# Low parts of x before the second layer norm, GpSimd taking over small work, and the hidden layer's tail cast on ScalarE

## What is computed

```python
xn = layernorm(x)                                   # over the 256 features
# recurrent branch (D = L = 256, K = 4 taps)
y    = gelu(xn @ w_y + b_y)
xb   = xn @ w_x + b_x
conv = conv_b + sum_k conv_w[k] * shift(xb, K-1-k)
gate_x = sigmoid(conv @ w_ig + b_ig); gate_a = sigmoid(conv @ w_ag + b_ag)
log_a = -8 * gate_a * softplus(a_param); a = exp(log_a); mult = sqrt(1 - exp(2*log_a))
h[t] = a[t] * h[t-1] + gate_x[t] * conv[t] * mult[t]    # a = 0, mult = 1 at t = 0
attn = (h * y) @ w_out + b_out
# feed-forward branch, HIDDEN = 682; ternary(w): -s, 0 or s with s = mean |w|
ffn  = (silu(xn @ ternary(w1)) * (xn @ ternary(w3))) @ ternary(w2)
out  = x + attn + ffn
```

## Time and profile before

| what | us |
|---|---|
| median of 3 runs (lowest, highest) | 75.48 (75.25, 76.12) |
| the profiled execution, its own time | 75.99 |
| its span, first to last instruction | 74.2 |

### The profile page before, as it was taken

One profiled execution on the slowest core, in us unless ns is written; L12 is line 12 of the kernel. 1 busy time (PEld: TensorE's weight loads), 2 busy tenths in 40 slices (PEclk: granted clock), 3 DMA queues, 4 the chain that ended last, 5 costly groups with the idle time before them and its releaser, 6 DMA issues.

```text
span 74.2 us, 1064 instructions
## 1 busy us (share of the span) xinstructions
PE 69.2 (93%) x364; PEld 58.6 (79%) x364; DVE 61.2 (82%) x101; ACT 48.3 (65%) x75; POOL 31.5 (43%) x43
## 2 busy tenths in 40 slices
PE   4999969999999999999999999999999999999920
PEld 4985758877888888888888888888899999988800
DVE  4897499999999999999979974697960799999750
ACT  3674523899999999999998978466699910000000
POOL 6385647245851680016002979947689000000000
PEclk9999999999999999999999999999999999999999
DMA  0889999920000000000000000000000000000195
...
DMA packets 5095, 5.63 MB, mean 76 GB/s; under 512 B 525, under 2 KB 4578, under 8 KB 5090
## 3 DMA queue, kind: packets, MB, share of 16 engines
...
q10 hardware_dynamic: 144, 0.01, 0.1%
...
HBM read 4.51 MB, written 1.05 MB: 75 GB/s over the span
## 4 chain that ended last, share of the span: by engine, by line
PE 80%; DMA 7%; DVE 5%; SPq 3%; issue 1%; DVEq 0%
PE slot L664 25%; PE slot L647 23%; PE slot L696 14%; PE slot L706 8%; DMA x_sb<-x 7%; PE slot L767 4%; PE slot L673 2%; SPq L186 2%; DVE stats L436 2%; PE slot L740 2%; DVE x_sb L551 1%; PE slot L636 1%; DVE xt_lo L455 1%; SPq L183 1%; DVEq L52 0%
## 5 line engine op out<-in xcount | busy, mean ns | idle before, releaser
L256 POOL TENSOR_TENSOR g_lo<-w_raw,g_hi 128x512 fp32r<-128x512 f32 x10 | 14.1, 1421 | 9.0 <-ACT g_hi L338 8.9
L664 PE MATMUL slot<-xt_hi,w_q 128*128 128x512 f32 x40 | 15.7, 393 | 0.0
L664 PE MATMUL slot<-xt_lo,w_q 128*128 128x512 f32 x40 | 15.7, 393 | 0.0
L514 DVE SCALAR_TENSOR_TENSOR w_raw<-w_raw,s,slot 128x512 f32<-128x512 f32 x10 | 7.3, 747 | 3.1 <-ACT w_raw L332 3.0
L696 PE MATMUL slot<-w_q,g_hi 128*128 128x256 f32 x40 | 9.7, 283 | 0.0
L696 PE MATMUL slot<-w_q,g_lo 128*128 128x256 f32 x40 | 9.7, 283 | 0.0
L492 DVE SCALAR_TENSOR_TENSOR conv<-slot,par,conv 128x511 f32<-128x511 f32 (+2 forms) x12 | 9.0, 748 | 0.4
L664 PEld LDWEIGHTS slot<-xt_hi,w_q 128*128 128x128 f32 x40 | 7.5, 188 | 1.7
L664 PEld LDWEIGHTS slot<-xt_lo,w_q 128*128 128x128 f32 x40 | 7.5, 188 | 1.7
L332 ACT ACTIVATE w_raw<-slot,scale 128x512 f32<-128x512 f32 x10 | 6.6, 684 | 3.1 <-PE slot L664 3.1
L696 PEld LDWEIGHTS slot<-w_q,g_lo 128*128 128x128 f32 x40 | 7.7, 192 | 0.0
...
## 6 DMA issues: line engine op xcount, KB each, us to landing
...
```

The source lines that it names most:

```text
L256: nc.gpsimd.tensor_tensor(g_lo[:, j, s], g[:, n % RING], g_hi[:, j, s].bitcast(f32), ALU.subtract).then_inc(g_lo_set, 1)
L514: nc.vector.scalar_tensor_tensor(out=g[:, n % RING], in0=silu[:, n % RING], scalar=s32[:, 0:1], in1=slot[H_SLOT[s][j]][:, 1], op0=ALU.mult ...
L664: mm = nc.tensor.matmul(slot[H_SLOT[s][j]][:, o], w13_q[:, c, col:col + P], v[:, s, c], start=(c == 0 and v is xt_hi), stop=(c == KC - 1 a ...
```

## The change

- SyncE loads sequence 1's x in two transfers instead of one.
- VectorE does `xt_lo_of(0)` ahead of sequence 1's statistics, takes that sequence in two halves, and puts the first columns of the convolution (`first_columns`, with constants of their own, in place of the correction L488) between the two normalisations and ahead of the taps. It no longer sets the pads of gt, makes v_eps or a_rate, or casts the tail.
- GpSimd makes v_eps, fewer constants ahead of the first rstd, the high parts of w_ig and w_ag (`tensor_copy`), w_y's low part in two chunks after all of xn, the rates, the pads, and b_split's low part after lo_of_g(4).
- ScalarE loads gelu's table by a one-column gelu ahead of w_y's high part, no longer makes the high parts of w_ig and w_ag, does conv_hi(0,0) behind both |w| sums, gate_x(0) ahead of conv_hi(1,1), the two tail casts (after g_hi(2) and after g_hi(5)) and b_split after g_hi(4).
- TensorE interleaves X(0)'s terms by halves, takes Y(0)'s hi and xt_lo terms first, then the transposes of sequence 1, then w_y's low terms by chunk; two warm-up matmuls with waits become one short one.

```diff
             for t in range(TILES):
                 sp.dma_start(x_sb[:, 0, t], x_dram[0][:, t]).then_inc(x_loaded[t], 16)
             square(WX)
-            sp.dma_start(x_sb[:, 1], x_dram[1]).then_inc(x_loaded[TILES], 16)
+            for i in range(2):
+                t = slice(i * TILES // 2, (i + 1) * TILES // 2)
+                sp.dma_start(x_sb[:, 1, t], x_dram[1][:, t]).then_inc(x_loaded[TILES + i], 16)
...
+            def square_hi(m):
+                pool.wait_ge(w_loaded[m], 16)
+                nc.gpsimd.tensor_copy(w_hi[:, m], w_raw[:, m]).then_inc(w_hi_set, 1)
+            def square_lo(m, chunks=range(KC)):
                 pool.wait_ge(w_hi_set, m + 1)
-                nc.gpsimd.tensor_tensor(w_lo[:, m], w_raw[:, m], w_hi[:, m].bitcast(f32), ALU.subtract).then_inc(w_lo_set, 1)
+                c = slice(chunks.start, chunks.stop)
+                nc.gpsimd.tensor_tensor(w_lo[:, m, c], w_raw[:, m, c], w_hi[:, m, c].bitcast(f32), ALU.subtract).then_inc(w_lo_set, len(chunks))
+            def rates():
+                pool.wait_ge(sp_log, 1)
+                nc.gpsimd.tensor_scalar(sp_e[:, 0], par[:, A_PARAM:A_PARAM + KC], 0.0, None, ALU.max).then_inc(rate_set, 1)
+                pool.wait_ge(rate_set, 1)
+                nc.gpsimd.tensor_tensor(sp_e[:, 1], sp_e[:, 0], sp_e[:, 2], ALU.add).then_inc(rate_set, 1)
+                pool.wait_ge(rate_set, 2)
+                nc.gpsimd.tensor_scalar(a_rate[:, :], sp_e[:, 1], -4.0, None, ALU.mult).then_inc(rate_set, 1)
             def rstd_of(s, tiles, ready):
+                pool.wait_ge(mv_set, TILES * s + tiles.stop)
+                nc.gpsimd.tensor_scalar(v_eps[:, s, tiles], mv[:, s, tiles, 1], EPS, None, ALU.add).then_inc(v_set, 1)
                 pool.wait_ge(v_set, ready)
                 pool.wait_ge(power_set, 1)
                 nc.gpsimd.tensor_tensor(rstd[:, s, tiles], v_eps[:, s, tiles], power[:, tiles], ALU.pow).then_inc(rstd_set, 1)
-            def conv_constants():
...
+            def tap_sum(i):
...
+                if i:
+                    pool.wait_ge(conv_c_set, i)
+                sum_so_far = conv_c[:, i - 1] if i else par[:, CONV_B:CONV_B + KC]
+                nc.gpsimd.tensor_tensor(conv_c[:, i], sum_so_far, b_tap[:, TAPS - 1 - i], ALU.add).then_inc(conv_c_set, 1)
...
+            def gt_pads(rows, value, chunk):
+                pool.wait_ge(conv_lo_set, chunk)
+                nc.gpsimd.memset(gt[rows].bitcast(f32), value).then_inc(gt_pads_set, 1)
...
-            conv_constants()
-            nc.gpsimd.tensor_scalar(half_b[:, :], par[:, B_IG:B_IG + 2 * KC], 0.5, None, ALU.mult).then_inc(half_b_set, 1)
+            tap_biases()
+            tap_sum(0)
             rstd_of(0, slice(0, TILES // 2), 1)
             rstd_of(0, slice(TILES // 2, TILES), 2)
+            for i in range(1, TAPS):
+                tap_sum(i)
             pool.wait_ge(xn_set, TILES)
             square_lo(WX)
-            rstd_of(1, slice(0, TILES), 3)
-            square_lo(WY)
-            square_lo(WIG)
-            square_lo(WAG)
-            for s in range(SEQS):
-                for c in range(KC):
-                    lo_of_conv(s, c)
-            pool.wait_ge(b_hi_set, 1)
-            nc.gpsimd.tensor_tensor(b_split[:, 1], b_row[:, :], b_split[:, 0].bitcast(f32), ALU.subtract).then_inc(b_split_set, 1)
+            rstd_of(1, slice(0, TILES // 2), 3)
+            rstd_of(1, slice(TILES // 2, TILES), 4)
+            pool.wait_ge(xn_set, 2 * TILES)
+            for c in range(KC):
+                square_lo(WY, range(c, c + 1))
+            for m in (WIG, WAG):
+                square_hi(m)
+                square_lo(m)
+            lo_of_conv(0, 0)
+            half_biases()
+            rates()
+            lo_of_conv(0, 1)
+            gt_pads(slice(32, HALF), 1.0, KC)
+            pool.wait_ge(gt_pads_set, 1)
+            lo_of_conv(1, 0)
+            gt_pads(slice(96, P), 0.0, KC + 1)
+            pool.wait_ge(gt_pads_set, 2)
+            lo_of_conv(1, 1)
             for n in range(2 * FULL):
                 lo_of_g(n)
+                if n == FULL - 1:
+                    pool.wait_ge(b_hi_set, 1)
+                    nc.gpsimd.tensor_tensor(b_split[:, 1], b_row[:, :], b_split[:, 0].bitcast(f32), ALU.subtract).then_inc(b_split_set, 1)
...
                 for c in range(KC):
-                    nc.scalar.activation(conv[:, s, c], slot[X_SLOT[s]][:, c], ACT.Identity,
+                    nc.scalar.activation(conv[:, s, c, k:], slot[X_SLOT[s]][:, c, k:], ACT.Identity,
                                          scale=par[:, CONV_W + KC * k + c:CONV_W + KC * k + c + 1],
-                                         bias=conv_c[:, 1, c:c + 1]).then_inc(tap_set, 1)
+                                         bias=conv_c[:, k, c:c + 1]).then_inc(tap_set, 1)
...
+            def tail_hi(dst):
+                act.wait_ge(g_t_set, 1)
+                act.wait_ge(gt_pads_set, 2)
+                nc.scalar.activation(dst.rearrange("p s n -> p (s n)"), g_t[HALF:HALF + TAIL], ACT.Copy).then_inc(gt_hi_set, 1)
...
             square_hi(WX)
             xt_hi_of(0)
+            act.wait_ge(quarter_set, 2)
+            nc.scalar.activation(gelu_in[:, 1:2], gelu_in[:, 0:1], ACT.Gelu)
             square_hi(WY)
             newest_tap(0)
-            square_hi(WIG)
             xt_hi_of(1)
             act.wait_ge(w1_loaded, 16)
             abs_sum_of(w13_raw[:, :, 0:HIDDEN], KC, junk_a, 0, abs13_set)
-            square_hi(WAG)
-            conv_hi_of(0, 0)
             act.wait_ge(w3_loaded, 16)
             abs_sum_of(w13_raw[:, :, W3_AT:W13], KC, junk_b, 1, abs13_set)
+            conv_hi_of(0, 0)
             newest_tap(1)
             conv_hi_of(0, 1)
             gelu_of(0)
             conv_hi_of(1, 0)
             gelu_of(1)
+            gate_x(0)
             conv_hi_of(1, 1)
-            gate_x(0)
...
             decays(0)
-            act.wait_ge(b_out_loaded, 16)
-            nc.scalar.activation(b_split[:, 0], b_row[:, :], ACT.Copy).then_inc(b_hi_set, 1)
...
-            act.wait_ge(w_lo_set, WIG + 1)
+            act.wait_ge(w_lo_set, KC * (WIG + 1))
             silu_of(0)
             silu_of(1)
...
             g_hi_of(2)
+            tail_hi(gt_hi[HALF:HALF + TAIL])
             silu_of(4)
             g_hi_of(3)
             g_hi_of(4)
+            act.wait_ge(b_out_loaded, 16)
+            nc.scalar.activation(b_split[:, 0], b_row[:, :], ACT.Copy).then_inc(b_hi_set, 1)
             for n in range(FULL, 2 * FULL):
                 silu_of(n)
                 if n > FULL:
                     g_hi_of(n - 1)
+                if n == FULL + 1:
+                    tail_hi(gt[0:TAIL])
             g_hi_of(2 * FULL - 1)
             for s in range(SEQS):
...
             nc.vector.memset(mult[:, :, :, 0:1], 0.5).then_inc(mult0_set, 1)
-            nc.vector.memset(gt[32:HALF].bitcast(f32), 1.0).then_inc(gt_pads_set, 1)
-            nc.vector.memset(gt[96:P].bitcast(f32), 0.0).then_inc(gt_pads_set, 1)
+            nc.vector.memset(gelu_in[:, 0:1], 0.0).then_inc(quarter_set, 1)
...
                     nc.vector.bn_aggr(mv[:, s, t], stats[:, s, t]).then_inc(mv_set, 1)
-                dve.wait_ge(mv_set, TILES * s + tiles.stop)
-                t = slice(tiles.start, tiles.stop)
-                nc.vector.tensor_scalar(v_eps[:, s, t], mv[:, s, t, 1], EPS, None, ALU.add).then_inc(v_set, 1)
...
+            def first_columns(s, c):
+                dve.wait_ge(conv_c_set, TAPS)
+                dve.wait_ge(tap_set, KC * s + c + 1)
+                k = TAPS - 1
+                nc.vector.scalar_tensor_tensor(
+                    out=conv[:, s, c, 0:k], in0=slot[X_SLOT[s]][:, c, 0:k],
+                    scalar=par[:, CONV_W + KC * k + c:CONV_W + KC * k + c + 1],
+                    in1=conv_c[:, 0:k, c], op0=ALU.mult, op1=ALU.add).then_inc(tap_step, 1)
...
             for i in range(2):
                 normalise(0, tile_halves[i], i + 1)
-            dve.wait_ge(x_loaded[TILES], 16)
-            statistics(1, range(TILES))
-            variance(1, range(TILES))
             xt_lo_of(0)
-            normalise(1, range(TILES), 3)
-            dve.wait_ge(sp_log, 1)
-            nc.vector.scalar_tensor_tensor(out=sp_e[:, 1], in0=par[:, A_PARAM:A_PARAM + KC], scalar=0.0, in1=sp_e[:, 2],
-                                           op0=ALU.max, op1=ALU.add).then_inc(rate_set, 1)
-            dve.wait_ge(rate_set, 1)
-            nc.vector.tensor_scalar(a_rate[:, :], sp_e[:, 1], -4.0, None, ALU.mult).then_inc(rate_set, 1)
+            for i in range(2):
+                dve.wait_ge(x_loaded[TILES + i], 16)
+                statistics(1, tile_halves[i])
+                variance(1, tile_halves[i])
+            normalise(1, tile_halves[0], 3)
+            first_columns(0, 0)
+            normalise(1, tile_halves[1], 4)
             older_taps(0, 0)
             xt_lo_of(1)
+            first_columns(0, 1)
             older_taps(0, 1)
```

(44 more changed lines are left out.)

72 lines of the change are left out of this document (29 added, 43 removed).

## The result

| what | before | after |
|---|---|---|
| median of 20 runs each (lowest, highest), us | 75.73 (75.25, 76.34) | 75.21 (74.63, 75.53) |
| the profiled execution, its own time | 75.99 | 75.14 |
| its span | 74.2 | 73.3 |

The ratio is 0.9934, with a 95% interval of 0.991 to 0.9958. The change gains 0.5 us; 74.5 was forecast, 0.7 lower. The profiled pair differs by 0.85 in time and 0.9 in span, near the 1.0 of my sum, and the medians by 0.52. Most of the study is about the gap between these two.

A forecast was written before the change was run, and what follows sets the result against it. TensorE, with matmuls in flight 93% of the span, was taken as the bound. Head 0.8, second stall 0.27, ring 0 to -0.1 made 1.0 us: 75.99 to 75.0, less 0.5 to the median, 74.5; range 74.0 to 75.6.

The forecast's parts named there:

- my sum: Whole kernel: 0.8 from the start, 0.27 from the stall at 17.68, 0 to -0.1 from the ring: 1.0 us gained.
- Head: Start of the kernel up to X(1): X(1) starts at 14.9, 0.8 us earlier.
- the first normalisation: Sequence 0, GpSimd and VectorE: rstd of the halves at 5.1 and 6.15, xn ends at 7.0 instead of 7.40.
- Second stall: TensorE's 0.31 us wait at 17.68 for sequence 1's `xt_lo`: it goes, worth about 0.27 us.
- Gelu's table: ScalarE's early table load, 8.1 to 9.4: w_y's high part ready at 10.25, hidden with 0.25 us to spare.
- The case of a late load: Rival at ScalarE's early table load: it costs twice the row, w_y's high part at 11.6, 0.3 lost, 74.8; chance 0.06.
- GpSimd up to the first gate: GpSimd from 14.3: new copies 0.8 each, conv_lo(0,1) ends at 22.25, 0.45 us before the gate asks at 22.7.
- Ring: VectorE's casts go to ScalarE, `tail_lo` ahead of g(5): g(5) ends 48.25, hidden(8) due 48.6; effect 0 to -0.1 us.
- the scans keep their distance: End of the ring: last g_hi ends at 54.8, 0.9 us earlier, about as much as TensorE, so scans don't fall behind.

The follow-up runs named there:

- a_tail_on_dve: Kernel after with both tail casts back on VectorE behind g(5), `tail_lo` behind g(7): median 75.81 us, ratio 1.0009 to the kernel before.
- b_tail_on_act: Kernel before with only the tail's casts on ScalarE and `tail_lo` ahead of g(5): 76.52 us, ratio 1.0157; repeated, 75.78 us, ratio 1.0006.
- b_tail_lo_old: Kernel before with the tail's casts on ScalarE but `tail_lo` at its old place behind g(7): 76.53 us, ratio 1.0104.

## Why the prediction was right or wrong

**Head.** Right in mechanism, near in size. `xt_lo(0)` was forecast at 7.1 and 8.2 and stood at 7.47 and 8.46. The normalisations ended at 12.9 (12.75 forecast), each chunk took 0.73 (0.75, of 0.65 to 1.3), and X(1) started at 15.04 (14.9): 0.67 gained for the 0.8 of the sum. What was late is GpSimd's run of v_eps and power, 10.12 to 12.15, where I had 9.9 to 11.9, and that goes back to the first normalisation. I had rstd of sequence 0's second half at 6.15, by GpSimd's own steps. It came at 6.53, since it needs the variance of that half, and VectorE had this at 5.34 only, behind the wait for the last tile (and at 5.32 in the kernel before: with the 1.0 of v_eps and power behind it, nothing before 6.3 was to be had).

**Second stall.** Right: the first gate moved 0.95, so 0.28 beside the 0.67, for the 0.27 forecast.

**Gelu's table.** Right: the load stood from 8.45 to 9.73, the high part ended at 10.47, Y(0) started at 10.71. The case of a late load did not happen. The Trainium skill (ScalarE: Activation LUTs, "What ACT_TABLE_LOAD costs") counts a drain of about 1.38 us more a switch. The trace does not agree here: the next activation starts 1.29 after the load does.

**GpSimd up to the first gate.** Right, with more cover: the copies took 0.63 and 0.61, not 0.8, and `conv_lo(0,1)` ended at 22.18 (22.25 forecast). By the Trainium skill (GPSIMD Engine Reference, "3.1 Elementwise — side-by-side cycle accounting") I had estimated 0.44 to 0.77 plus dispatch; the trace agrees.

**Ring.** Right in the walk, near in size. g(5) stood from 47.77 to 48.5 (47.5 to 48.25 forecast), and hidden(8) did not wait. What I had not seen is how little "the scans keep their distance" meant: the distance is 0.1 us. And I had costed the casts on ScalarE against their own kernel only. Left on VectorE they are a stall of 0.54, as `a_tail_on_dve` shows, since they then lie beside GpSimd's subtractions.

**Sum.** The profiled pair gives 0.85 for my 1.0. The step that failed is the one behind the sum: "That execution is 0.5 above the median of 75.48; a gain on the path counts the same there, so the forecast is 74.5." The gain does not count the same there. The change takes the wait for sequence 1's x off the path, and in the execution that I predicted from this x landed late (8.34). I used the landing as a fixed number, and the runs show that it moves: 7.74 and 8.37 for the start of the statistics in two profiles of one kernel, with the span moving by as much, and a forced delay that costs the kernel before 1.0 us and the kernel after nothing.

The error of 0.7 (74.48 before rounding) falls into three parts. 0.15 is the sum, 0.85 for 1.0. 0.25 is that the median of the 3 executions shown was 75.48 where 20 gave 75.73. 0.33 is the gap between the profiled pair and the medians: the profiled execution of the kernel before lay 0.26 above its median, that of the kernel after 0.07 under. That the 0.26 is the landing is an estimate: on its line a median of 75.73, less the 1.8 around the span, is a start of the statistics near 8.1, but an unprofiled run shows no landing. In an execution with x in at 7.4, about when VectorE first asks, the line gives a span of 73.2 for the kernel before, within 0.1 of the kernel after's profiled 73.3. So against that profile the gain is 0.9 with the late landing and close to nothing with the earliest, with 0.5 between; unprofiled executions of the kernel before have been seen with a span of 73.3.

The parts, by the runs: the guard on GpSimd about 0.3, the casts 0.5 to 0.7 in the presence of the rest and nothing of their own that three runs of the kernel before could show, the two transfers nothing, the early table nothing, v_eps on GpSimd a loss of 0.1 to 0.2 in the profile that the ratio doesn't show. They don't add up to the whole, because each is measured with the others in place. Open are the first result of `b_tail_on_act`, which its repetition did not give again, the spread of 2 us in `b_tail_lo_old`, and how much of the spread of either kernel each landing makes.
